# Seven block products in place of eight for the attention values, and dense weights loaded by pairs of chunks

## What is computed

```python
x = x + attn(layernorm(x))
#   y = conv1d(x, 3 taps, 1024 -> 3*256) + b ; q, k, v = split(y)
#   blocks of 128 tokens, 16 heads of 64:  qh = q @ wq + bq ; kh = k @ wk + bk ; vh = v @ wv + bv
#   p = softmax(causal(qh * scale @ kh.T)) ; o = (p @ vh) @ wo + bo ; o @ proj_w + proj_b
x = x + ffn(layernorm(x))
#   y = x @ W_base.T + b_base, plus low-rank terms of 4 experts weighted by a softmax gate
```

## Time and profile before

| | before |
|---|---|
| median of 3 runs | 769.10 us (769.08 to 769.15) |
| the profiled execution | 769.19 us |
| its span, first to last instruction | 767.4 us |
| TensorE (PE) busy | 749.3 us, 98% of the span |
| VectorE (DVE) busy | 552.6 us, 72% |
| ScalarE (ACT) busy | 452.5 us, 59% |
| GpSimd (POOL) busy | 173.2 us, 23% |
| chain that ended last | PE 92%, DVE 3%, ACT 2% |
| mean granted clock of TensorE | 0.998 of 2.4 GHz |

### The profile page before, as it was taken

The page is one execution under the profiler, slowest core; times in us unless marked ns, Lnnn a source line. Parts: engine busy times, 40 slices in busy tenths (PEclk is TensorE's granted clock), DMA queues, the critical chain, the costliest instruction groups (busy, mean ns, idle before and its releaser), DMA issues.

```text
span 767.4 us, 15056 instructions
## 1 busy us (share of the span) xinstructions
PE 749.3 (98%) x5326; PEld 673.8 (88%) x5326; DVE 552.6 (72%) x1503; ACT 452.5 (59%) x1180; POOL 173.2 (23%) x204
## 2 busy tenths in 40 slices
PE   4999999999999999999999999999999999999997
PEld 3898888888888888999898999999989899999997
DVE  6999996879888875656556555456588567777774
ACT  5963433334433788687777787777794155566530
POOL 2300100000000124525162626252430201222200
PEclk9999999999999999999999999999999999999999
DMA  8846833444445345442525160702057976333402
GB/s 326 297 118 192 255 121 125 172 164 145 163 151 206 111 167 144 146 174 72 195 71 186 37 227 18 232 1 111 1 195 221 364 216 204 133 121 137 160 29 83
DMA packets 61246, 118.86 MB, mean 155 GB/s; under 512 B 11507, under 2 KB 30067, under 8 KB 59892
## 3 DMA queue, kind: packets, MB, share of 16 engines
q1 hardware_dynamic: 59156, 110.56, 43.0%
q0 software_dynamic: 2016, 7.34, 2.3%
HBM read 82.68 MB, written 34.80 MB: 153 GB/s over the span
## 4 chain that ended last, share of the span: by engine, by line
PE 92%; DVE 3%; ACT 2%; issue 1%; DMA 1%; DVEq 0%; POOL 0%; ACTq 0%; POOLq 0%
PE net_psum L63 15%; PE net_psum L65 15%; PE net_psum L64 15%; PE net_psum L1791 11%; PE net_psum L2033 5%; PE net_psum L2035 5%; PE net_psum L2034 5%; PE net_psum L1853 4%; PE net_psum L1864 4%; PE net_psum L1876 4%; PE net_psum L1906 2%; PE net_psum L1907 2%; PE net_psum L1908 2%; PE net_psum L1775 1%; ACT pr L888 1%
## 5 line engine op out<-in xcount | busy, mean ns | idle before, releaser
L719 POOL TENSOR_TENSOR pr<-pr,rrec 128x512 f32<-128x512 f32 x64 | 66.5, 1040 | 209.2 <-DVE rrec L1328 206.0
L888 ACT ACTIVATE pr<-pr,negmax 128x128 f32<-128x128 f32 x256 | 99.0, 395 | 1.0 <-DVE negmax L1320 1.0
L1791 PE MATMUL net_psum<-ua,wa 128*128 128x256 f32 x384 | 83.8, 379 | 0.6 <-DVE ua L1210 0.6
L1791 PEld LDWEIGHTS net_psum<-ua,wa 128*128 128x128 f32 x384 | 72.6, 190 | 10.4 <-issue 0.8
L1320 DVE CUSTOM_DVE_ANT_0 pr<-net_psum,mask 128x128 f32<-128x128 f32 x256 | 57.0, 286 | 29.6 <-PE net_psum L1853 29.6
L63 PE MATMUL net_psum<-x_hi,w_hi 128*128 128x512 f32 x192 | 76.4, 398 | 0.0
L64 PE MATMUL net_psum<-x_lo,w_hi 128*128 128x512 f32 x192 | 76.2, 397 | 0.0
L845 ACT ACTIVATE w_hi<-raw 128x1024 fp32r<-128x1024 f32 x24 | 25.5, 1062 | 85.5 <-PE net_psum L65 76.8
L65 PE MATMUL net_psum<-x_hi,w_lo 128*128 128x512 f32 x192 | 75.6, 393 | 0.0
L63 PE MATMUL net_psum<-c_hi,wqk_hi 128*128 128x256 f32 x256 | 74.1, 290 | 0.0
L64 PE MATMUL net_psum<-c_lo,wqk_hi 128*128 128x256 f32 x256 | 71.6, 280 | 0.0
(11 more groups left out here) (268 smaller groups left out, 2257.4 us busy)
## 6 DMA issues: line engine op xcount, KB each, us to landing
wa<-in_conv_w SPq DMA_DIRECT2D x24, 512.0 KB, 4.2
raw<-in_conv_w SPq DMA_DIRECT2D x24, 384.0 KB, 4.2
xn<-in_x SPq DMA_DIRECT2D x16, 512.0 KB, 10.2
xr<-in_x SPq DMA_DIRECT2D x8, 1024.0 KB, 5.6
x_scratch<-xr SPq DMA_DIRECT2D x8, 1024.0 KB, 4.4
x1t<-x_scratch SPq DMA_DIRECT2D x16, 512.0 KB, 5.1
x1g<-x_scratch SPq DMA_DIRECT2D x56, 128.0 KB, 3.0
out<-x1t POOLq DMA_DIRECT2D x14, 512.0 KB, 3.0
```

The lines of the kernel that those rows point to most:

```text
L719: pool.tensor_tensor(pr[:, jj % 4], pr[:, jj % 4], rrec[:, jj % 4].unsqueeze(2).to_broadcast([P, UN, P]), ALU.mult).then_inc(s["p_ready"], 1)
L888: e = act.activation(pr[:, jj % 4, un], pr[:, jj % 4, un], ACT.Exp, bias=negmax[:, jj % 2, un:un + 1], scale=-1.0, accum_out=rsum[:, jj % ...
L1791: mm = pe.matmul(duo_acc(d, mi)[:, v * QUADS:(v + 1) * QUADS], wa[:, a % AW, mi, 1 - v, c % 2], ua[:, c, v, n * QUADS:(n + 1) * QUADS], st ...
```

## The change

From group 2 on (`SEVEN = 2`) the values of a group are computed as a 2 x 2 by 2 x 2 block product with seven block products in place of eight. A block of c is 128 tokens by 128 channels, a block of wv is 128 by 512. Four sums of blocks of c are made per group by VectorE from `c_raw` (`value_sums`, q = 3 of the group before), split by ScalarE (`vs_hi`, at the end of that step) and VectorE (`low_values`, q = 0). Four sums of blocks of wv are made once, by VectorE in step 5 (`value_weight_sums`), from a second copy of wv (`wv_again`, loaded by SyncE in the first attention step); ScalarE splits three of them in step 5 and the fourth in step 6, over a block of `wv_hi`; VectorE makes their low parts in steps 6 (`low_value_sums`) and 7 (`low_last_sum`). ScalarE's split in step 5 waits for all four sums; the one in step 6 waits for the last values of group 1.

The seven products are three matmuls each. Products 1 and 2 take the place of the first unit of step 4g + 1, product 3 that of its second unit; 4 and 5, 6 and 7 are the two units of step 4g + 2. Products 3, 5, 6 and 7 accumulate onto what stands in their bank, and wait until VectorE has copied the earlier content; VectorE makes seven copies or additions into `vf` in place of four. `head_outputs` of a group waits for all seven.

The dense weights are no longer loaded whole before step 8: the place in SBUF is used by the sums for the values. A pair of chunks (`w_pair`) is loaded for each four weight sums, and the gate's columns are written into it (`gate_weights(n)`). Four chunks are loaded again after the last sum, the other four once TensorE has finished the last value product (step 30); `gate_weights` for these stands at the end of VectorE's step 31, and `high_dense` waits for it.

The core of the diff (declarations, and the count functions of semaphores, left out in part):

```diff
+    SEVEN = 2
+    V_SUMS = WC + 4
+    def v_before(e):
+        return VT * min(e, SEVEN) + 7 * max(0, e - SEVEN)
+    def v_left(e, n, k):
+        return v_before(e) + ((n + 1) if e < SEVEN else ((3, 2), (7, 6))[n // 2][k])
+    def v_low(e):
+        return V_SUMS + 4 + 5 * (e - SEVEN)
...
+        w_pair, = place(nc, RAW, (("w_pair", [P, 2, WZ], F32),))
+        vs_hi, vs_lo = place(nc, RAW + 2 * size_of([P, WZ]), (("vs_hi", [P, 4, P], F32R), ("vs_lo", [P, 4, P], F32R)))
+        vs_raw, = place(nc, RAW + 2 * size_of([P, WZ]) + size_of([P, 4, P]), (("vs_raw", [P, 4, P], F32),))
+        vt_hi, vt_lo = place(nc, RAW + 3 * size_of([P, WZ]), (("vt_hi", [P, 3, BANK], F32R), ("vt_lo", [P, 3, BANK], F32R)))
+        wv_again, = place(nc, XL + 6 * CHUNK + size_of([P, DM]), (("wv_again", [P, WC, HW_], F32),))
...
+            def load_weights(*rows):
+                for to, c in rows:
+                    for (lo, hi), off, (left, right) in zip(COLS, OFF, OUT):
+                        sync.dma_start(to[:, lo + off:lo + off + right - left], w_base[:, c, left:right]).then_inc(s["fw_loaded"], 16)
...
+                    if g + 1 >= SEVEN:
+                        sync.wait_ge(s["v_low_step"], v_low(g + 1) + 4)
...
+                    sync.dma_start(wv_again[:], wv).then_inc(s["wv_loaded"], 16)
...
-                    for c in range(DC):
-                        for (lo, hi), off, (left, right) in zip(COLS, OFF, OUT):
-                            sync.dma_start(fw_raw[:, row(c), lo + off:lo + off + right - left], w_base[:, c, left:right]).then_inc(s["fw_loaded"], 16)
+                    load_weights(*((w_pair[:, row(c) // 4], c) for c in (0, 4)))
+                if 1 < g <= TSUMS // 4 and i == 5:
+                    sync.wait_ge(s["t_step"], sum_step(4 * (g - 1) - 1))
+                    load_weights(*((w_pair[:, row(c) // 4], c) for c in (g - 1, g + 3)))
+                if (g, i) == (TSUMS // 4 + 1, 6):
+                    sync.wait_ge(s["t_step"], sum_step(TSUMS - 1))
+                    load_weights(*((fw_raw[:, row(c)], c) for c in range(4)))
                 if (g, i) == (8, 0):
+                    sync.wait_ge(s["v_done"], v_before(NG))
+                    load_weights(*((fw_raw[:, row(c)], c) for c in range(4, DC)))
...
+                if D == 5:
+                    act.wait_ge(s["v_low_step"], V_SUMS)
+                    for i, block in enumerate((value_block(0, 0), value_block(1, 1), value_block(0, 1))):
+                        act.activation(vt_hi[:, i], block, ACT.Copy).then_inc(s["v_high_ready"], 1)
+                if D == 6:
+                    act.wait_ge(s["v_done"], v_before(SEVEN))
+                    act.activation(wv_hi[:, 0, BANK:2 * BANK], value_block(1, 0), ACT.Copy).then_inc(s["v_high_ready"], 1)
+                if q == 3 and SEVEN <= g + 1 < NG:
+                    act.wait_ge(s["v_low_step"], v_low(g + 1) + 4)
+                    act.activation(vs_hi[:], vs_raw[:], ACT.Copy).then_inc(s["v_high_ready"], 1)
...
+                act.wait_ge(s["t_step"], gates_step(TSUMS // 4 + (c >= 4)))
...
+            def value_out(e, step, i, j, bank):
+                to = vf[:, i, j * BANK:(j + 1) * BANK]
+                dve.wait_ge(s["v_done"], v_before(e) + step)
+                if step in (1, 3, 4, 7):
+                    dve.tensor_copy(to, vy[bank]).then_inc(s["v_ready"], 1)
+                else:
+                    dve.wait_ge(s["v_ready"], v_before(e) + step - 1)
+                    dve.tensor_tensor(to, vy[bank], to, ALU.add).then_inc(s["v_ready"], 1)
+            def value_weight_sums():
+                b11, b12, b21, b22 = value_block(0, 0), value_block(0, 1), value_block(1, 0), value_block(1, 1)
+                dve.wait_ge(s["wv_loaded"], 32)
+                for k, (to, left, right) in enumerate(((b11, b12, b11), (b12, b22, b12), (b22, b22, b11), (b21, b21, b22))):
+                    dve.wait_ge(s["v_low_step"], WC + k)
+                    dve.tensor_tensor(to, left, right, ALU.subtract).then_inc(s["v_low_step"], 1)
+            def low_value_sums():
+                for i, block in enumerate((value_block(0, 0), value_block(1, 1), value_block(0, 1))):
+                    dve.wait_ge(s["v_high_ready"], WC + i + 1)
+                    dve.tensor_tensor(vt_lo[:, i], block, vt_hi[:, i], ALU.subtract).then_inc(s["v_low_step"], 1)
+            def low_last_sum():
+                dve.wait_ge(s["v_high_ready"], WC + 4)
+                dve.tensor_tensor(wv_lo[:, 0, BANK:2 * BANK], value_block(1, 0), wv_hi[:, 0, BANK:2 * BANK], ALU.subtract).then_inc(s["v_low_step"], 1)
+            def value_sums(e):
+                a11, a12, a21, a22 = c_block(c_raw, 0, 0), c_block(c_raw, 0, 1), c_block(c_raw, 1, 0), c_block(c_raw, 1, 1)
+                s1, s2, s3, s4 = (vs_raw[:, i] for i in range(4))
+                dve.wait_ge(s["c_loaded"], 16 * e)
+                dve.tensor_tensor(s1, a21, a22, ALU.add).then_inc(s["v_low_step"], 1)
+                dve.tensor_tensor(s3, a11, a21, ALU.subtract).then_inc(s["v_low_step"], 1)
+                dve.wait_ge(s["v_low_step"], v_low(e) + 1)
+                dve.tensor_tensor(s2, s1, a11, ALU.subtract).then_inc(s["v_low_step"], 1)
+                dve.wait_ge(s["v_low_step"], v_low(e) + 3)
+                dve.tensor_tensor(s4, a12, s2, ALU.subtract).then_inc(s["v_low_step"], 1)
+            def low_values(e):
+                dve.wait_ge(s["v_high_ready"], WC + 4 + e - SEVEN + 1)
+                dve.tensor_tensor(vs_lo[:], vs_raw[:], vs_hi[:], ALU.subtract).then_inc(s["v_low_step"], 1)
...
+                if is_v and e >= SEVEN:
+                    if D % DG == 1 and k == 0:
+                        value_out(e, 1, 0, 0, 0)
+                        value_out(e, 2, 0, 0, 1)
+                    elif D % DG == 2 and k == 0:
+                        value_out(e, 4, 1, 1, 1)
+                        value_out(e, 5, 1, 1, 0)
+                    elif D % DG == 2:
+                        value_out(e, 6, 0, 1, 1)
+                        value_out(e, 7, 1, 0, 0)
...
+                if q == 2 and SEVEN <= g < NG:
+                    dve.wait_ge(s["o_done"], 2 * (D - PV) + 2)
+                    value_out(g, 3, 0, 1, 0)
+                if D == 7:
+                    low_last_sum()
+                if q == 3 and SEVEN <= g + 1 < NG:
+                    value_sums(g + 1)
...
-                if D == TFIRST - 1:
-                    gate_weights()
                 weight_sums(D, True)
+                if TFIRST - 1 <= D < sum_at(TSUMS) - 1 and q == 3:
+                    gate_weights((D + 1 - TFIRST) // DG)
+                if D == W_LAST:
+                    gate_weights(TSUMS // 4)
+                if D == ND - 1:
+                    gate_weights(TSUMS // 4 + 1)
+                if D == 5:
+                    value_weight_sums()
+                if D == 6:
+                    low_value_sums()
+                if q == 0 and SEVEN <= g < NG:
+                    low_values(g)
...
+            def gate_weights(n):
+                pair = n < TSUMS // 4
+                dve.wait_ge(s["fw_loaded"], 16 * NB * (2 * n + 2 if pair else 2 * TSUMS // 4 + (4 if n == TSUMS // 4 else DC)))
+                if n == 0:
+                    dve.wait_ge(s["az_loaded"], 64 * E_ACT)
+                for rows, chunks in (((w_pair, slice(row(n) % 4, row(n) % 4 + 5, 4)),) if pair else
+                                     ((fw_raw[:, 6:8], slice(6, 8)), (fw_raw[:, 0:2], slice(0, 2))) if n == TSUMS // 4 else
+                                     ((fw_raw[:, 2:6], slice(2, 6)),)):
+                    dve.memset(rows[:, :, 3 * QW - PAD:3 * QW + PAD], 0.0)
+                    half, two = ER // 2, E_ACT // 2
+                    for h in range(2):
+                        dve.tensor_copy(rows[:, :, QW * h:QW * h + half], a_raw[:, chunks, half * h:half * h + half])
+                        z = dve.tensor_copy(rows[:, :, QW * h + half:QW * h + ZW], r_raw[:, two * h:two * h + two, chunks].rearrange("p e c -> p c e"))
                 z.then_inc(s["t_step"], 1)
...
+                b11, b12 = w_pair[:, row(c) // 4, 0:2 * QW], w_pair[:, row(c) // 4, 2 * QW:WZ]
+                b21, b22 = w_pair[:, row(c + 4) // 4, 0:2 * QW], w_pair[:, row(c + 4) // 4, 2 * QW:WZ]
...
+                dve.wait_ge(s["t_step"], sum_step(k - 1) if k % 4 else gates_step(c))
...
+            def value_product(bank, x_hi, x_lo, w_hi, w_lo, first):
+                pe.matmul(vy[bank], x_hi, w_hi, start=first, stop=False, skip_group_check=True)
+                pe.matmul(vy[bank], x_hi, w_lo, start=False, stop=False, skip_group_check=True)
+                pe.matmul(vy[bank], x_lo, w_hi, start=False, stop=True, skip_group_check=True).then_inc(s["v_done"], 1)
+            def seven_values(D, k, e):
+                at = v_before(e)
+                c = lambda i, j: (c_block(c_hi[e % 2], i, j), c_block(c_lo[:, e % 2], i, j))
```

(71 more changed lines are left out.)

21 lines of the change are left out of this document (8 added, 13 removed).

## The result

| | before | after |
|---|---|---|
| median of the runs | 769.10 us | 780.12 us (779.26 to 780.43) |
| ratio, 95% interval | | 1.0141 (1.0124 to 1.0159) |
| the profiled execution | 769.19 us | 779.26 us |
| its span | 767.4 us | 777.5 us |
| TensorE busy, matmuls | 749.3 us, 5326 | 747.2 us, 5308 |

What follows compares the result with a forecast made beforehand. The prediction took TensorE, busy for 98% of the span, to bound the kernel. Its terms -0.7 + 2.4 + 7.5 + 1.5 = +10.7 us on 769.2 gave 779.9, say 779.8 us, range 768 to 783.5.

Steps and rivals of the forecast that it cites:

- the 4.15 us of 18 matmuls: Groups 2 to 7: 18 fewer wide matmuls at 0.23 us, 4.15 us if nothing takes it back; forecast saving 0.7 us.
- the long one: TensorE's wait for a_lo at projection(0, 0) in step 7, forecast 7.5 us, plus 1.5 us for half clock behind it.

## What to carry to other kernels

- When an engine that bounds the kernel gets less work, look at what it waits for next, a step later: the 4.15 us of 18 matmuls were worth 0.7 us until one operation ahead of the next wait was moved, and 2.7 us then.
- One-time work of the setting up belongs in time in which its engine idles, not into a full run ahead of something that the bounding engine waits for. Seven subtractions moved so gave back 11.4 us (780.1 to 768.7), and nothing was left out.
- Price VectorE operations with two inputs in SBUF by what GpSimd does at that moment, and price a wait of TensorE together with the clock that it may lose.

## What the runs showed of the hardware

- VectorE and GpSimd took turns, one operation each, where both had subtractions or sums with two SBUF inputs queued (steps 6 and 7): three subtractions took 1175, 2310 and 2870 ns beside c_lo and the bias sums, and 681 to 684 ns alone.
- A wait of TensorE of 2.1 to 2.2 us was followed by half clock (0.50 to 0.54 in the stretch from 302 to 304) in three of four profiled executions, and by full clock (1.00) in the fourth. I had expected it only from the long one. Behind the long one (6.56 us) the half clock cost 1.6 us.
- Fifty-six transposes of the identity, 0.11 us each (6.04 us from the first to the next matmul), kept the clock at 1.00 through a wait. It is of use only where the wait can't be removed.
